# Zero matmuls left out beside the FFN and the prep stage, two loads moved in SyncE's order, a new table of steps

## The chip, the cores and the metric

The kernel runs on one NeuronCore of a Trainium2 chip. The metric is the device time of one execution in microseconds (us); lower is better. All arithmetic is float32 except where bf16 is named.

## The reference, cut to what matters

The model is one hybrid block over `x` of shape (8, 512, 256), that is 8 batch items of 512 positions:

```
x = x + attn(layernorm(x))                      # 16 heads, rotary, causal
x = x + ffn(layernorm(x))                       # FP4-quantised inputs and weights, F = 704
h = layernorm(x)
x = x + (h + mamba(layernorm(h)*gamma + beta))  # two directions, 512 channels, 16 states
x = x + ffn(layernorm(x))                       # the same weights again

# mamba, for each direction:
xc = silu(conv4(xs));  dt = softplus(...)
state = exp(dt*A)*state + dt*B*xc;  y = sum_n state_n*C_n + xc*D     # a scan over 512 positions
y = concat(y_fwd, y_back) @ merge_w * silu(z) @ out_w
```

The scan is the largest single part: 2 directions x 4 tiles of 128 channels x 16 states of a 512-long recurrence for each of 8 batch items.

## The kernel before

**Two streams.** The main stream is the scan. It is cut into units: a unit `K` is two states of one 128-channel tile, so 64 units a block (a block is one batch item) and 512 in all. Per unit ScalarE makes two tiles of factors (L1312), GpSimd the products `dBu` (L1027), VectorE two scans (L891) and two products with C (L898), and TensorE sums the states in a PSUM bank with an identity matmul (`state_sum`, L1614; a float32 matmul is recorded as two instructions). In some units GpSimd adds the two states first (L1038). SyncE spreads the rows of B and C over the 128 partitions for every unit (L544, L556, two transfers of 512 KB).

The side stream is all the rest, for the blocks next door: in the time of block `b` run, in this order, `merge` (end of mamba of block b-1, and the first statistics of item b+1), `ffn` of b-1 (the second FFN, "ffn2"), `latents`, `attention` and `ffn` of item b+1 ("ffn1"), and `prep` of item b+1 (the projection, convolution and inputs of its scan). Each engine has a generator for this side stream; a step of it is a *visit*, the same number on every engine. `VISITS` says how many visits are done at each half unit; `pace(b)` joins the lists of the stages, and each engine's main loop calls `advance(side, visits[2k])` and `advance(side, visits[2k+1])` in unit `k`. Every engine runs its instructions in program order, so this table is the order of the work. The lists give `merge` 5 units, `ffn2` 6, `lat` 8, `att` 22, `ffn1` 5.5, `early` 6.5 (the first 20 visits of prep), and `late` the last 7 visits of prep. After them the block's remaining units run with nothing beside them.

**Zero matmuls.** On TensorE `keep_busy()` (L1359) issues one bf16 matmul of a zero weight tile (`zerob`) with 512 columns, accumulated into the bank of the state sum, so that it adds nothing. It is called once a visit of `ffn` (53 visits) and of `prep` (27 visits), while a state sum is open (`summing[0]`).

**Loads.** SyncE issues all transfers in one queue and waits in order. At visit 0 of `merge` it waits for the stores of the last prep, then loads the input of the next item into `xin` (L471), the gate `yg` (L473) and the residual `x` (L474). VectorE needs `xin` at visit 1 of merge (`tile_stats`, L628), `yg` at visit 3 (L667) and `x` at visit 13 (L674). In `prep` SyncE stores the residual at visit 6 (L497, after GpSimd made it), `xc` of the two directions at 16 and 20 (L504), the gate at 20 (L500), and the dt inputs at 23 and 26 (L510). VectorE's work in an FFN tile runs from the product of gate and up (L705), which waits for TensorE's up matmul, through the quantisation (L595 to L625), to the addition of the result (L726), which waits for the down matmul.

Of the kernel before, what the change touches and what calls it, by code (L numbers as in the profile page):

```python
# [18 lines left out]
BF16 = mybir.dt.bfloat16  # L19
I32 = mybir.dt.int32  # L20

P = 128
B, T, C = 8, 512, 256
TT = T // P
# [16 lines left out]
NP, NQ = 2 * DT, DS // 2  # L41
# [6 lines left out]
YB = 2  # L48
# [94 lines left out]
def mixed_with(i):  # L143
# [6 lines left out]
PREP_EARLY = 20  # L150
EARLY_MERGE = (26, 34, 42, 50, 58)
VISITS = {
    "merge": (1, 1, 1, 1, 0, 5, 0, 2, 2, 5),
    "ffn2": (1, 1, 9, 1, 10, 8, 3, 5, 3, 4, 4, 4),
    "lat": (4, 0, 1, 1, 0, 3, 1, 1, 0, 2, 0, 3, 2, 2, 0, 6),
    "att": (0, 4, 1, 0, 2, 0, 3, 0, 5, 1, 1, 0, 2, 2, 0, 0, 2, 3, 1, 1, 1, 1,
            3, 4, 2, 1, 1, 0, 2, 0, 1, 1, 1, 0, 3, 1, 3, 5, 0, 4, 0, 0, 0, 3),
    "ffn1": (2, 5, 6, 8, 9, 8, 0, 7, 4, 1, 3),
    "early": (4, 1, 2, 1, 2, 0, 5, 1, 1, 0, 3, 0, 0),
    "late": (2, 0, 2, 0, 0, 0, 0, 1, 0, 0, 2, 0, 0, 0, 0),  # L160
}


# [25 lines left out]
def hybrid_block(nc, known, d, out):  # L189

    with ExitStack() as ctx:
        def sb(name, shape, dt=F32):
            return ctx.enter_context(nc.sbuf_tensor("sb_" + name, shape, dt))
# [9 lines left out]
        identb = sb("identb", [P, P], BF16)  # L203
        maskb = sb("maskb", [P, P], BF16)
        cos, sin = sb("cos", [P, T]), sb("sin", [P, T])
        ones = sb("ones", [L + 1, P])
        zerob = sb("zerob", [P, P], BF16)
        e16 = sb("e16", [1, 17])
        w_lat = [[sb(f"w_lat{w}{r}", [P, CK, HL]) for r in range(2)] for w in range(2)]
        b_lat = sb("b_lat", [P, 2 * 2 * MT])  # L210
# [65 lines left out]
        lat = [area(MT, T, start=W), area(MT, T)]  # L276
# [170 lines left out]
        def _(sp):  # L447
# [9 lines left out]
            def merge(c, n):  # L457
                latest = min((c + 2 if n is None else n) - 1, B - 1)
                for v in range(MERGE_N):
                    if v == 0 and c != B - 1:  # L460
                        if latest >= 0:
                            done = 16 * (latest + 1)
                            sp.wait_ge(s_kept_x, done)
                            sp.wait_ge(s_kept_zs, done)
                            for s in range(2):
                                sp.wait_ge(s_kept_xc[s], done)
                                sp.wait_ge(s_kept_z[s], done)
                                sp.wait_ge(s_rows[s], done)
                        if n is not None and n >= 1:
                            sp.wait_ge(V.sem, V.at("attended", n - 1, TT - 1))  # L470
                            sp.dma_start(xin[:, :, :], x_dram[n]).then_inc(s_xin, 16)  # L471
                        if c is not None:
                            sp.dma_start(yg, kept_zs[c]).then_inc(s_yg, 16)  # L473
                            sp.dma_start(x[:, :, :], kept_x[c]).then_inc(s_x, 16)  # L474
                    yield

            def last_loads():
                store_out(B - 2)
# [13 lines left out]

            def prep(n):
                for v in range(PREP_N):
                    if v == 6:
                        sp.wait_ge(G.sem, G.at("residual", n))
                        sp.dma_start(kept_x[n], x[:, :, :]).then_inc(s_kept_x, 16)  # L497
                    if v == 20:
                        sp.wait_ge(A.sem, A.at("z", n, DT - 1))
                        sp.dma_start(kept_zs[n], zs).then_inc(s_kept_zs, 16)  # L500
                    for s, at_xc, at_rows, at_z in ((0, 16, 18, 23), (1, 20, 23, 26)):
                        if v == at_xc:
                            sp.wait_ge(A.sem, A.at("xc", n, s, DT - 1))
                            sp.dma_start(kept_xc[n, s], xc[s]).then_inc(s_kept_xc[s], 16)  # L504
                        if v == at_rows:
                            sp.wait_ge(A.sem, A.at("xds", n, s))
                            sp.dma_start(rows_bc[n, s], xds[s][DR:XD]).then_inc(s_rows[s], 16)
                        if v == at_z:
                            sp.wait_ge(A.sem, A.at("zraw", n, s, DT - 1))
                            sp.dma_start(kept_z[n, s], zraw[s]).then_inc(s_kept_z[s], 16)  # L510
                    yield
# [78 lines left out]
        def _(v):  # L590
# [239 lines left out]
            after(V.n)  # L830
            for r in range(4):
                v.memset(own_rows[L * r:L * r + L, r:r + 1], 1.0).then_inc(V.sem, V.mark())
            v.memset(zerob[:, :], 0.0).then_inc(V.sem, V.mark())
            v.memset(minus_one[:, :], -1.0).then_inc(V.sem, V.mark())
            v.memset(minus_half[:, :], -0.5).then_inc(V.sem, V.mark("cleared"))
            v.wait_ge(s_fold, FOLD)
# [504 lines left out]
        def _(pe):  # L1341
# [9 lines left out]
                if name:  # L1351
                    mm.then_inc(E.sem, E.mark(*name))

            summing = [False]

            def keep_busy():

                if summing[0]:
                    pe.matmul(psum[:, YB], zerob[:, :], identb[:, :].unsqueeze(1).to_broadcast([P, T // P, P]),  # L1359
                              start=False, stop=False)  # L1360

            def merge_tiles(c, first, end):
                for k in range(first, end):
                    pe.wait_ge(V.sem, V.at("ycat", c * NP + k))
# [31 lines left out]

            def ffn(b, f):
                for i in range(FFN_N):
                    keep_busy()
                    for w, first in ((0, 7), (1, 12)):  # L1400
                        if i == first:
                            pe.wait_ge(G.sem, G.at("xq", b, f, w))
# [150 lines left out]

            def prep(n):
                for i in range(PREP_N):
                    keep_busy()
                    if i in (5, 6):
                        k = i - 5
                        pe.wait_ge(A.sem, A.at("normed3", n, TT - 1))
# [42 lines left out]
            def state_sum(K):  # L1602
# [11 lines left out]
                    mm = pe.matmul(psum[:, YB], ident[:, :], dBu[K % SLOTS][:, e],  # L1614
                                   start=(q == 0 and e == 0), stop=(q == NQ - 1 and e == last))
                mm.then_inc(E.sem, E.mark("summed", K))
                summing[0] = q < NQ - 1


            pe.wait_ge(s_fold, FOLD)  # L1620
# [115 lines left out]
```

## Time and profile before

| | |
|---|---|
| median of 3 runs | 3912.75 us (3910.37 to 3913.55) |
| profiled execution, its own time | 3910.42 us |
| its span | 3908.6 us |
| TensorE busy | 3340.3 us (85%), of it the zero matmuls 266.7 us in 842 instructions |
| VectorE busy | 2988.5 us (76%) |
| GpSimd busy | 2136.8 us (55%) |
| ScalarE busy | 1992.6 us (51%) |
| mean granted TensorE clock | 0.945 |

The profiled execution lies 2.3 us below the median, and 1.8 us of it lie outside the span. Matmuls are pipelined, and their busy time contains latency: the distance from start to start is what one of them takes from TensorE. The first scan unit starts at 311.7 us; blocks 1 to 6 start at 717.6, 1179.7, 1642.3, 2104.6, 2571.9 and 3036.9 us, block 7 at 3500.8 us, and its last unit at 3821.2 us. "The granted clock" is a share of the full 2.4 GHz; its two levels are 1 and 0.5.

### The profile page before, as it was taken

The page shows a single profiled execution, that of the slowest core. Times are in us where ns is not written, and L with a number is a line of the kernel's source. Part 1 is how long each engine was busy: PE and PEld are TensorE (multiplying, and loading weights), DVE is VectorE, ACT ScalarE, POOL GpSimd, SP SyncE. Part 2 cuts the span into 40 slices and gives each one's busy share as a digit, 9 for nine tenths or more (in the row PEclk, how much of TensorE's full clock was granted, in tenths as well). Part 3 has the DMA queues.
Part 4 walks back from the last instruction along what each step waited for, and adds up shares of the span by engine and source line. Part 5 has one row for each costly group of instructions (what it writes and reads, how often), then busy time and mean ns, then how long its engine had stood idle before and what let it go on. Part 6 is the DMA issues. An engine that isn't in the chain of part 4 may idle for free.

```text
span 3908.6 us, 40355 instructions
## 1 busy us (share of the span) xinstructions
PE 3340.3 (85%) x12858; PEld 1747.6 (45%) x12858; DVE 2988.5 (76%) x4258; ACT 1992.6 (51%) x3811; POOL 2136.8 (55%) x1333
## 2 busy tenths in 40 slices
PE   7877988899888988889888998889988898889676
PEld 4543543355434554355443454435543455435223
DVE  5346788786887778877887878878688777887885
ACT  2544656346553565545654466534655356553442
POOL 2016566556654665546745466555665466553881
PEclk9988999899999999999999999999999999999888
DMA  3006446644464543734537344464446445373880
GB/s 91 1 28 230 150 136 235 223 146 148 143 239 165 164 162 139 281 112 165 184 116 278 129 148 165 175 224 146 148 142 238 166 159 162 131 283 114 280 273 29
DMA packets 203667, 649.30 MB, mean 166 GB/s; under 512 B 34237, under 2 KB 45504, under 8 KB 197312
## 3 DMA queue, kind: packets, MB, share of 16 engines
q1 hardware_dynamic: 203456, 646.72, 48.8%
q8 instruction: 103, 1.69, 0.2%
q14 instruction: 108, 0.88, 0.1%
HBM read 595.26 MB, written 51.38 MB: 165 GB/s over the span
## 4 chain that ended last, share of the span: by engine, by line
PE 34%; issue 21%; POOL 20%; DVE 16%; ACT 5%; DMA 3%; SPq 1%; POOLq 0%; DVEq 0%; ACTq 0%
PE banks L1345 15%; POOL sb_arena L1027 9%; PE banks L1614 7%; DVE banks L891 5%; PE banks L1385 4%; POOL sb_arena L1038 3%; PE banks L1350 3%; PE banks L1537 3%; DVE sb_arena L898 2%; DVE sb_arena L802 2%; POOL sb_arena L962 2%; ACT banks L1312 2%; POOL sb_arena L939 1%; PE banks L1513 1%; DMA sb_xin<-in_x 1%
## 5 line engine op out<-in xcount | busy, mean ns | idle before, releaser
L1027 POOL TENSOR_TENSOR sb_arena<-sb_arena 128x1024 f32<-128x1024 f32 x512 | 1205.6, 2356 | 364.3 <-DMA sb_arena<-rows_bc 200.3
L891 DVE TENSOR_TENSOR_SCAN banks<-banks,sb_arena 128x512 f32<-128x512 f32 x999 | 1170.0, 1215 | 155.6 <-ACT banks L1312 108.8
L1312 ACT ACTIVATE banks<-sb_arena,sb_neg_a 128x512 f32<-128x512 f32 x1024 | 665.4, 682 | 1014.3 <-DVE sb_arena L898 1003.4
L1614 PE MATMUL banks<-sb_arena,sb_ident 128*128 128x512 f32 x1740 | 915.4, 646 | 277.3 <-DVE sb_arena L898 162.3
L898 DVE TENSOR_TENSOR sb_arena<-banks,sb_arena 128x512 f32<-128x512 f32 x999 | 635.6, 676 | 2.8 <-DMA sb_arena<-rows_bc 2.8
L1614 PEld LDWEIGHTS banks<-sb_arena,sb_ident 128*128 128x128 f32 x1740 | 324.2, 201 | 700.3 <-DVE sb_arena L898 276.9
L1081 ACT ACTIVATE sb_arena<-banks 128x512 f32<-128x512 f32 (+2 forms) x720 | 360.9, 515 | 535.2 <-PE banks L1350 380.8
L1350 PE MATMUL banks<-sb_ident,sb_arena 128*128 128x128 f32 (+1 forms) x2082 | 343.2, 287 | 194.3 <-POOL sb_arena L932 74.0
L756 DVE TENSOR_REDUCE sb_nmax<-banks 128x1 f32<-128x512 f32 (+3 forms) x352 | 223.7, 636 | 270.3 <-PE banks L1540 269.5
L1350 PEld LDWEIGHTS banks<-sb_ident,sb_arena 128*128 128x128 f32 (+1 forms) x2082 | 241.0, 144 | 407.1 <-ACT sb_arena L1081 158.0
L1537 PE MATMUL banks<-sb_arena 128*128 128x384 f32 (+3 forms) x1024 | 353.2, 455 | 1.9 <-POOL sb_arena L949 1.9
L1345 PE MATMUL banks<-sb_w_gu,sb_arena 128*128 128x352 f32 x1024 | 352.8, 493 | 1.5 <-ACT sb_arena L1081 1.5
L939 POOL TENSOR_TENSOR sb_arena<-sb_arena,sb_q_s 128x704 f32<-128x704 f32 x64 | 88.8, 1387 | 477.9 <-DVE sb_arena L625 477.9
L1038 POOL TENSOR_TENSOR sb_arena<-sb_arena 128x512 f32<-128x512 f32 x154 | 195.3, 1268 | 229.6 <-DVE sb_arena L898 227.7
L1157 ACT ACTIVATE sb_arena<-banks,sb_nmax 128x512 f32<-128x512 f32 (+3 forms) x512 | 264.6, 527 | 20.2 <-DVE sb_nmax L756 19.9
L1359 PE MATMUL banks<-sb_identb,sb_zerob 128*128 128x512 bf16 x842 | 266.7, 405 | 0.0
L1345 PEld LDWEIGHTS banks<-sb_w_gu,sb_arena 128*128 128x128 f32 x1024 | 204.6, 204 | 128.3 <-issue 28.6
L1345 PE MATMUL banks<-sb_arena,sb_w_lat 128*128 128x512 f32 x512 | 235.6, 602 | 8.5 <-DVE sb_arena L743 7.8
L1345 PE MATMUL banks<-sb_w_down,sb_arena 128*128 128x256 f32 (+1 forms) x768 | 201.5, 405 | 12.3 <-ACT sb_arena L1081 7.8
L1385 PE MATMUL banks<-sb_arena,sb_w_merge 128*128 128x512 f32 x448 | 196.8, 592 | 0.0
L1513 PE MATMUL banks<-sb_arena 128*32 128x128 f32 x2560 | 183.2, 277 | 6.5 <-ACT sb_arena L1081 6.3
L962 POOL TENSOR_TENSOR sb_arena<-sb_arena,sb_own_rows 128x1024 f32<-128x1024 f32 x64 | 121.3, 1895 | 122.2 <-PE banks L1540 117.7
(130 smaller groups left out, 4102.5 us busy)
## 6 DMA issues: line engine op xcount, KB each, us to landing
sb_arena<-rows_bc SPq DMA_DIRECT2D x1024, 512.0 KB, 4.5
kept_xc<-sb_arena SPq DMA_DIRECT2D x16, 1024.0 KB, 7.6
kept_z<-sb_arena SPq DMA_DIRECT2D x16, 1024.0 KB, 7.5
sb_arena<-kept_xc SPq DMA_DIRECT2D x64, 256.0 KB, 5.1
sb_arena<-kept_z SPq DMA_DIRECT2D x63, 256.0 KB, 5.0
kept_zs<-sb_arena SPq DMA_DIRECT2D x8, 1024.0 KB, 8.6
sb_arena<-kept_zs SPq DMA_DIRECT2D x8, 1024.0 KB, 9.4
sb_xin<-in_x SPq DMA_DIRECT2D x8, 512.0 KB, 7.3
```

Source lines behind the costliest of these rows:

```text
L891: v.tensor_tensor_scan(products if e == 1 and shared(K) else factors, factors, products, 0.0, ALU.mult, ALU.add).then_inc(V.sem, V.mark("s ...
L898: v.tensor_tensor(dBu[K % SLOTS][:, e], psum[:, e], rows_c[K % CS][:, e], ALU.mult).then_inc(V.sem, V.mark("hc", K, e))
L1027: nc.gpsimd.tensor_tensor(dBu[K % SLOTS], u[:, p % 2].unsqueeze(1).to_broadcast([P, 2, T]), rows_b[K % BS], ALU.mult).then_inc(G.sem, G.ma ...
L1038: nc.gpsimd.tensor_tensor(dBu[K % SLOTS][:, 0], dBu[K % SLOTS][:, 0], dBu[K % SLOTS][:, 1], ALU.add).then_inc(G.sem, G.mark("pair", K))
L1081: nc.scalar.activation(dst, src, ACT.Copy).then_inc(A.sem, A.mark(*name))
L1312: nc.scalar.activation(psum[:, e], dt[:, (K // NQ) % 2], ACT.Exp, scale=neg_a[:, s, m, 2 * q + e:2 * q + e + 1]).then_inc(A.sem, A.mark("d ...
L1345: mm = pe.matmul(dst, lhs, rhs, start=(i == 0), stop=(i == len(pairs) - 1))
L1350: mm = pe.transpose(dst, src, ident[0:src.shape[0], 0:src.shape[0]])
L1359: pe.matmul(psum[:, YB], zerob[:, :], identb[:, :].unsqueeze(1).to_broadcast([P, T // P, P]), start=False, stop=False)
L1385: mm = pe.matmul(psum[:, SB[j]], w_merge[:, k, j * P:j * P + P], ycat[:, k], start=(k == 0), stop=(k == 2 * DT - 1))
L1537: pe.matmul(psum[:, bank, e * kl:e * kl + kl], qz[:, m, r], lat[1][:, m, 0:kl], start=(e == 0), stop=False)
L1614: mm = pe.matmul(psum[:, YB], ident[:, :], dBu[K % SLOTS][:, e], start=(q == 0 and e == 0), stop=(q == NQ - 1 and e == last))
```

## The change

The zero matmuls go (TensorE, and the memset of `zerob` on VectorE). The load of `xin` for item n+1 goes from visit 0 of `merge` to visit 0 of `prep(n)`, for the items 2 to 7 (item 1 is still loaded in merge). The load of the residual goes from visit 0 of `merge` to visit 14 of `prep(n)` one block earlier, behind a wait for the store of the newer residual from the same tile. The lists of `VISITS` are other; each stage has as many visits and takes as many half units as before, except that `late` spreads its 7 visits over 8 half units and not 15.

```
 VISITS = {
-    "merge": (1, 1, 1, 1, 0, 5, 0, 2, 2, 5),
-    "ffn2": (1, 1, 9, 1, 10, 8, 3, 5, 3, 4, 4, 4),
-    "lat": (4, 0, 1, 1, 0, 3, 1, 1, 0, 2, 0, 3, 2, 2, 0, 6),
-    "att": (0, 4, 1, 0, 2, 0, 3, 0, 5, 1, 1, 0, 2, 2, 0, 0, 2, 3, 1, 1, 1, 1,
-            3, 4, 2, 1, 1, 0, 2, 0, 1, 1, 1, 0, 3, 1, 3, 5, 0, 4, 0, 0, 0, 3),
-    "ffn1": (2, 5, 6, 8, 9, 8, 0, 7, 4, 1, 3),
-    "early": (4, 1, 2, 1, 2, 0, 5, 1, 1, 0, 3, 0, 0),
-    "late": (2, 0, 2, 0, 0, 0, 0, 1, 0, 0, 2, 0, 0, 0, 0),
+    "merge": (1, 1, 0, 3, 4, 1, 1, 0, 1, 6),
+    "ffn2": (1, 1, 7, 3, 9, 9, 4, 3, 8, 0, 4, 4),
+    "lat": (4, 0, 2, 2, 0, 3, 0, 3, 2, 0, 1, 1, 1, 4, 1, 2),
+    "att": (0, 3, 2, 0, 2, 0, 3, 0, 5, 1, 1, 0, 2, 1, 1, 0, 2, 3, 1, 1, 1, 1,
+            3, 4, 2, 1, 1, 1, 1, 0, 1, 1, 1, 1, 2, 1, 3, 5, 0, 2, 2, 0, 0, 3),
+    "ffn1": (2, 7, 3, 9, 9, 8, 0, 7, 6, 0, 2),
+    "early": (4, 1, 3, 0, 2, 0, 7, 0, 0, 0, 3, 0, 0),
+    "late": (2, 0, 2, 1, 0, 1, 0, 1),
 }
...
-        zerob = sb("zerob", [P, P], BF16)
...
-                        if n is not None and n >= 1:
-                            sp.wait_ge(V.sem, V.at("attended", n - 1, TT - 1))
-                            sp.dma_start(xin[:, :, :], x_dram[n]).then_inc(s_xin, 16)
+                        if n == 1:
+                            load_x(n)
                         if c is not None:
                             sp.dma_start(yg, kept_zs[c]).then_inc(s_yg, 16)
-                            sp.dma_start(x[:, :, :], kept_x[c]).then_inc(s_x, 16)
+            def load_x(n):
+                sp.wait_ge(V.sem, V.at("attended", n - 1, TT - 1))
+                sp.dma_start(xin[:, :, :], x_dram[n]).then_inc(s_xin, 16)
...
             def prep(n):
                 for v in range(PREP_N):
+                    if v == 0 and 1 <= n < B - 1:
+                        load_x(n + 1)
+                    if v == 14 and n >= 1:
+                        sp.wait_ge(s_kept_x, 16 * (n + 1))
+                        sp.dma_start(x[:, :, :], kept_x[n - 1]).then_inc(s_x, 16)
                     if v == 6:
                         sp.wait_ge(G.sem, G.at("residual", n))
                         sp.dma_start(kept_x[n], x[:, :, :]).then_inc(s_kept_x, 16)
...
-            def keep_busy():
-                if summing[0]:
-                    pe.matmul(psum[:, YB], zerob[:, :], identb[:, :].unsqueeze(1).to_broadcast([P, T // P, P]),
-                              start=False, stop=False)
...
             def ffn(b, f):
                 for i in range(FFN_N):
-                    keep_busy()
...
             def prep(n):
                 for i in range(PREP_N):
-                    keep_busy()
```

## Rows read from the trace of the kernel before

**Rows 1.** Windows, one line a block: busy us and count of each engine, clock, DMA.

```profile
717.60:1179.70 462.10, 410.91 (x1602) 216.03 (x1602) 370.26 (x528) 247.04 (x472) 263.95 (x165) 0.96 0.50 173
2104.60:2571.90 467.30, 412.76 (x1602) 216.38 (x1602) 370.24 (x528) 246.89 (x473) 265.52 (x165) 0.96 0.51 171
```

**Rows 2.** Windows of block 3: merge, ffn2, lat, att, ffn1, early, late, last units.

```profile
core 0: us, PE busy (x) PEld busy (x) DVE busy (x) ACT busy (x) POOL busy (x), PEclk, DMA share, GB/s
1642.30:1680.00 37.70, 36.14 (x84) 15.89 (x85) 22.73 (x37) 10.26 (x16) 18.66 (x11) 1.00 0.70 252
...
1752.00:1799.00 47.00, 47.00 (x122) 22.12 (x123) 37.84 (x48) 19.94 (x34) 33.10 (x21) 1.00 0.63 212
...
2013.00:2063.00 50.00, 41.56 (x104) 17.47 (x105) 42.13 (x63) 35.06 (x55) 25.64 (x16) 0.93 0.60 198
...
2084.00:2104.60 20.60, 10.40 (x24) 3.40 (x21) 19.43 (x24) 9.29 (x15) 16.77 (x10) 1.00 0.92 321
```

**Rows 3.** Windows of the merge stages of blocks 1 to 6, and their sum.

```profile
717.60:753.60 36.00, 36.00 (x84) 15.94 (x85) 22.74 (x37) 10.22 (x16) 17.29 (x11) 1.00 0.70 254
...
2104.60:2145.40 40.80, 37.75 (x84) 16.59 (x85) 22.87 (x37) 10.29 (x16) 18.95 (x11) 0.96 0.68 239
...
sum 227.10, PE 218.63 PEld 96.32 DVE 136.80 ACT 61.73 POOL 111.80; mean PE 36.44 PEld 16.05 DVE 22.80 ACT 10.29 POOL 18.63
```

**Rows 4.** Timeline of VectorE, TensorE and SyncE at the start of block 3.

```profile
1645.49 0.38 SPq L471 DMA_DIRECT2D sb_xin<-in_x  x1
...
1653.50 0.75 DVE L628 BATCH_NORM_STATS2 sb_stats<-sb_xin 128x6 f32<-128x256 f32 x2 [6.27 <-DMA sb_xin<-in_x]
...
1650.91 5.31 PE L1385 MATMUL banks<-sb_arena,sb_w_merge 128*128 128x512 f32 x12
1657.78 1.98 PE L1614 MATMUL banks<-sb_arena,sb_ident 128*128 128x512 f32 x4 [1.56 <-DVE sb_arena L898]
```

**Rows 5.** The instructions on the tile `xin`: what they waited for.

```profile
  DMA sb_xin<-in_x: 42.5, 8
```

**Rows 6.** Windows of ffn2 (first three) and of ffn1 in four blocks.

```profile
1216.60:1288.00 71.40, 61.51 (x231) 36.82 (x229) 59.97 (x96) 30.76 (x47) 24.03 (x16) 0.98 0.27 89
1680.00:1751.80 71.80, 61.91 (x231) 37.05 (x229) 60.00 (x96) 30.76 (x47) 24.04 (x16) 0.95 0.26 88
...
2609.70:2682.60 72.90, 64.70 (x231) 37.86 (x230) 60.04 (x97) 30.78 (x47) 24.03 (x16) 0.93 0.26 87
...
1946.20:2012.10 65.90, 58.74 (x206) 32.67 (x206) 56.66 (x91) 31.82 (x48) 30.41 (x23) 0.87 0.30 98
2412.70:2479.20 66.50, 57.45 (x206) 32.43 (x206) 56.72 (x91) 31.82 (x48) 30.47 (x23) 0.92 0.29 96
```

**Rows 7.** Windows of the zero matmuls alone, in ffn2, ffn1 and early.

```profile
1680.00:1751.80 71.80, 12.42 (x42) 4.14 (x42) 0.95 0.26 88
...
1946.20:2012.10 65.90, 16.80 (x50) 5.34 (x50) 0.87 0.30 98
...
2012.10:2062.30 50.20, 6.57 (x21) 2.10 (x21) 0.93 0.60 199
```

**Rows 8.** Timeline of TensorE in FFN stretches.

```profile
1961.35 4.13 PE L1345 MATMUL banks<-sb_w_gu,sb_arena 128*128 128x352 f32 x8
1965.31 0.59 PE L1359 MATMUL banks<-sb_identb,sb_zerob 128*128 128x512 bf16 x2
1965.74 2.53 PE L1345 MATMUL banks<-sb_w_gu,sb_arena 128*128 128x352 f32 x8
1968.11 0.38 PE L1359 MATMUL banks<-sb_identb,sb_zerob 128*128 128x512 bf16 x1
...
1486.51 3.19 PE L1359 MATMUL banks<-sb_identb,sb_zerob 128*128 128x512 bf16 x7
```

**Rows 9.** Groups of VectorE in block 3: busy, mean ns, idle before them.

```profile
L756 DVE TENSOR_REDUCE sb_nmax<-banks 128x1 f32<-128x384 f32 (+3 forms) x44 | 27.9, 634 | 30.6 <-PE banks L1540 30.4
...
L705 DVE TENSOR_TENSOR sb_arena<-sb_arena,banks 128x704 f32<-128x704 f32 x8 | 7.1, 885 | 8.3 <-PE banks L1345 8.3
...
L726 DVE TENSOR_TENSOR sb_x<-sb_x,banks 128x256 f32<-128x256 f32 x8 | 3.3, 418 | 4.9 <-PE banks L1345 4.8
```

**Rows 10.** Timeline of SyncE's queue in prep, block 3.

```profile
2023.53 0.32 SPq L497 DMA_DIRECT2D kept_x<-sb_x  x1
...
2048.34 0.32 SPq L556 DMA_DIRECT2D sb_arena<-rows_bc  x1
2048.71 1.26 SPq L504 DMA_DIRECT2D kept_xc<-sb_arena  x1
```

**Rows 11.** Transfers of the page and of the DMA view: KB each, us to landing.

```profile
kept_x<-sb_x SPq DMA_DIRECT2D x8, 512.0 KB, 4.5
```

More of the change, by code:

```diff
@@ L832, in _ @@
                 v.memset(own_rows[L * r:L * r + L, r:r + 1], 1.0).then_inc(V.sem, V.mark())
-            v.memset(zerob[:, :], 0.0).then_inc(V.sem, V.mark())
             v.memset(minus_one[:, :], -1.0).then_inc(V.sem, V.mark())
@@ L1352, in turn @@
                     mm.then_inc(E.sem, E.mark(*name))
-            summing = [False]
-            def keep_busy():
-                if summing[0]:
-                    pe.matmul(psum[:, YB], zerob[:, :], identb[:, :].unsqueeze(1).to_broadcast([P, T // P, P]),
-                              start=False, stop=False)
             def merge_tiles(c, first, end):
@@ L1616, in state_sum @@
                 mm.then_inc(E.sem, E.mark("summed", K))
-                summing[0] = q < NQ - 1
             pe.wait_ge(s_fold, FOLD)
```

## The prediction, as recorded before the change ran

> **What bounds the kernel now.** I read the windows by block first. Six middle blocks take 462 to 467 us each and hold the same work to within 2 us of VectorE time [rows 1]; so what is won or lost in a block counts about six or seven times. The windows by stage come next, because no engine bounds the whole [rows 2]. In merge TensorE is busy 36.1 of 37.7 us and VectorE only 22.7. In lat TensorE is busy all of 47.0 us. In the last units, with no side work, VectorE is busy 19.4 of 20.6 us and TensorE half. In the two FFN stretches both are near full: TensorE 58.7 and VectorE 56.7 of 65.9 us in ffn1, 61.9 and 60.0 of 71.8 in ffn2 [rows 6]. But TensorE's number there contains the zero matmuls, 16.8 and 12.4 us [rows 7]. Without them it is 41.9 of 65.9 and 49.5 of 71.8 us: there VectorE is the engine to beat, and TensorE matters only where VectorE stands waiting for it. That is read from the groups of VectorE: in a block it waits 8.3 us for up matmuls (L705) and 4.9 us for down matmuls (L726) [rows 9].
>
> **The change part by part.**
>
> *The zero matmuls.* In a run two of them take 0.59 us and one 0.38 us [rows 8], so one more costs 0.21 us of TensorE. In blocks 1 to 6 the two FFN stretches hold 92 of them a block (42 and 50) and early 21 [rows 7]. All of it together is 842 x 0.21 = 177 us, which would be the gain if TensorE set the pace everywhere; the rows above say it doesn't. What lies on the path is what stands, without a pause of TensorE, before a matmul for which VectorE waits. The pattern of a tile shows it: eight gate matmuls from 1961.35, two zeros from 1965.31 to 1965.74, eight up matmuls to 1968.27, and VectorE's L705 follows at once [rows 8]. So 0.43 us of such a wait is zeros. The down matmuls come after two rounds of transposes and copies, in whose pauses the zeros run at no cost. A block has 8 tiles; eight instructions of L705 wait 8.3 us in all [rows 9], and in the timeline all but about one of them do so: 7 x 0.43 = 3.0 us a block, and seven blocks have about this much FFN beside a scan: 21 us. The bounds: 0, if VectorE then waits for something else that is as late; and all of L705's and L726's waits, 13.2 x 7 = 92 us. I take 21, since the pattern is seen, with the zeros of early at 0: there VectorE is busy 42.1 of 50.0 us, TensorE 41.6 [rows 2], and the 21 zeros (4.5 us) mostly lie in TensorE's waits for the convolution. Bounded above by those 4.5 x 7 = 31 us.
>
> *The load of xin.* In block 3 SyncE issues it at 1645.49 and VectorE stands 6.27 us until 1653.50 [rows 4]. In the trace all such waits are 42.5 us in 8 times [rows 5], of which two (item 0 and item 1) stay. But merge is TensorE's stage: while VectorE stands, TensorE works on merge matmuls until 1656.22, and its own wait for VectorE's product is 1.56 us [rows 4]. The six merge stages say the same: the shortest is 36.0 us with TensorE busy all the time, the longest 40.8, and together they take 227.1 us, 11.1 more than six times the shortest [rows 3]. So the gain is 11 us, not the 36 or so of VectorE's waiting; 11 and 36 are the bounds, with 0 as the lower one should the transfer be late at its new place. It isn't: at visit 0 of prep SyncE's wait is for the last addition of attention, a whole FFN earlier, and 17.5 units lie between it and the next merge: early, late and the last units, over 90 us (2012.1 to 2104.6), against 8.0 us from issue to use before [rows 4].
>
> *The load of the residual.* It was in time before, at visit 13 of merge, so by itself it is worth nothing; that merge starts with 1 MB less in flight only helps `yg`. Its new place has a wait, and behind it in SyncE's queue stand the spreads of B and C for the next units, then GpSimd's products, then VectorE. The wait is for the store issued at visit 6, at 2023.53 [rows 10], which lands some 4.5 us later [rows 11]; visit 14 comes two units later. Long done: 0. The two transfers go into a stretch whose DMA share is 0.60 against merge's 0.70 [rows 2]. If they delayed the spreads by their own 8 us, a lead of three units or more (over 20 us here) would cover it. The new list for early puts visits 10 to 16 in one half unit, so SyncE waits for `xc` (L504, at 2048.71 before) ahead of the spreads of one more unit; it already stood until 2048.34 for a spread buffer [rows 10]. I take 0 and keep 1 us a block, 7 us, for it.
>
> *The clock.* This is what speaks against the change. A low clock costs: ffn2 takes 71.4 us at a mean of 0.98, 71.8 at 0.95 and 72.9 at 0.93; ffn1 takes 65.9 us at 0.87 and 66.5 at 0.92, so there it costs nothing visible [rows 6]. The slope in ffn2 is 1.5 us for 0.05. Fewer matmuls mean more idle time for TensorE, and in places nothing but zeros keeps it at work: seven in a row from 1486.51 [rows 8]. On the other side, in the last units of block 3 TensorE is busy half the time and the granted clock is 1.00 [rows 2], while the FFN stretches keep 64% and 69% without zeros. So I expect more falls, not a low stage: the mean in FFN stretches down by 0.03 to 0.04, which by ffn2's slope is 1.0 us each, 14 of them: 14 us lost. Bounds: 0 (ffn1's rows), and the slope applied to a fall of 0.12, 50 us.
> The Trainium skill (TensorE: Matmul & The Clock Gate, "HAM oscillation — how this bites in real kernels") speaks against the change: pauses of TensorE put it back to half clock, so that each burst starts cold. The trace agrees that falls happen beside FFN, but the stage means of 0.87 to 0.98 were had with the fillers in place. By the rule taken strictly, every FFN tile would begin cold; that is the third rival below.
>
> *The table.* Its stages keep their lengths, so the stage bounds stay; only the order inside moves, and `late` ends 1.5 units sooner, where VectorE is the bound and nothing waits. No row gives its price. The largest wait that such an order can touch is VectorE's for attention scores, 30.6 us a block [rows 9]. I take 1 us a block in favour, 7 us, because merge's new list brings TensorE's matmuls forward into the time in which VectorE no longer stands; the bounds are 15 us either way.
>
> The sum against the profiled execution: 3910.4 - 21 - 11 + 14 - 7 = 3885.4; the median of the runs shown is 2.3 us above it, so 3887.7. I forecast 3888 us, 0.6% less.
>
> **The rivals.**
> 1. *VectorE's waits in the FFN go nearly whole.* TensorE then runs ahead in the FFN, and the down matmuls are early too. For it speaks that TensorE has a third of the stretch free; against it, that down matmuls follow copies of ScalarE. Two thirds of the 92 us, 61 instead of 21, and the clock at 14: 3848. Chance 0.15.
> 2. *Nothing comes through.* The zeros ran only in pauses, and the merge stage keeps its length because TensorE was its bound (36.0 us at best). Then 3912.7 - 11 + 14 = 3916, and 3905 at least where the clock costs little and the table pays. Chance 0.17.
> 3. *The clock falls for much of the FFN* (slower). Place: both FFN stretches of every block, where TensorE waits for the quantised tile. It decides from a fall of the mean by 0.09: then 14 x 2.8 us eat the 39 us of all gains. At a fall of 0.12, 3.6 us each: 3912.7 - 39 + 50 = 3924. For it speak the seven zeros in a row, and the skill's rule; against it the half-busy last units at full clock. Chance 0.14.
> My forecast has 0.5; 0.04 is left for a late spread behind the new wait of visit 14, up to +15 us.
>
> **How the numbers follow.** The forecast's own range is 3868 to 3904. A measurement of this kernel tells 0.2%, 8 us, from no change: faster is below 3905, slower above 3920.5. Faster: 0.5 + 0.15 and 0.02 of rival 2, 0.67. Within: most of rival 2 and a part of the others, 0.18. Slower: 0.15. To leave out two in ten the range takes in half of rival 1 and half of rivals 2 and 3: 3848 to 3917.
>
> **What would show it.** Merge stages all near 36 us, without VectorE's wait for xin. FFN stretches 1 to 2 us shorter, L705's wait in a block down from 8.3 to about 5 us. Their granted clock 0.03 to 0.04 lower; at 0.80 rival 3 holds. Lat unchanged at 47 us. Wrong I would be by the table above all, since it has no price, and by the clock where slow matmuls fall on waits of VectorE.

## The result, and the profile after

The changed kernel takes 3952.35 us (median of 5 runs, 3948.61 to 3956.88) against 3912.75 us before (3910.37 to 3915.54 in its 5 runs beside it). The ratio is 1.0099, with a 95% interval of 1.0088 to 1.0111: 1.0% slower, where 3888 us and 0.6% less was forecast. The profiled execution has a span of 3946.8 us and a mean granted clock of 0.922; before it was 3908.6 us and 0.945.

First the windows by block, as in [rows 1] (columns: window and length, then busy us and count on TensorE, its weight loads, VectorE, ScalarE, GpSimd, then granted clock, DMA share, GB/s).

```profile
720.30:1186.80 466.50, 388.28 (x1480) 206.78 (x1480) 372.37 (x528) 247.06 (x472) 264.95 (x165) 0.94 0.50 171
...
1657.90:2129.60 471.70, 393.54 (x1481) 209.82 (x1481) 372.34 (x528) 247.24 (x473) 265.64 (x166) 0.92 0.50 170
```

TensorE has lost its ballast (388 to 394 us a block for 406 to 413), VectorE's work is 2 us more (372.4 for 370.2 in block 1), and yet a block takes 1.5 to 9.4 us more; the two shown, blocks 1 and 3, take 4.4 and 9.4. The six middle blocks sum to 2814.3 us (720.3 to 3534.6) for 2783.2 before (717.6 to 3500.8), so 31 of the 38 us of span lie there. The windows of block 3 by stage show where: merge, ffn2, lat, att, ffn1, early, late, last units.

```profile
1657.90:1693.90 36.00, 36.00 (x84) 16.05 (x85) 23.04 (x37) 10.34 (x17) 18.92 (x12) 1.00 0.62 232
1693.90:1767.80 73.90, 57.62 (x189) 35.09 (x187) 59.89 (x96) 30.77 (x47) 26.80 (x18) 0.88 0.28 98
1767.80:1823.50 55.70, 55.62 (x134) 26.64 (x135) 39.77 (x50) 19.94 (x35) 35.32 (x24) 0.91 0.50 164
1823.50:1966.20 142.70, 126.67 (x773) 75.96 (x771) 109.30 (x149) 97.42 (x241) 101.17 (x63) 0.99 0.51 167
1966.20:2033.00 66.80, 46.04 (x156) 27.70 (x156) 58.44 (x91) 31.60 (x48) 30.50 (x23) 0.87 0.30 97
2033.00:2083.90 50.90, 38.07 (x85) 16.81 (x85) 42.88 (x64) 34.45 (x54) 24.46 (x15) 0.87 0.65 207
2083.90:2105.30 21.40, 19.52 (x43) 7.12 (x41) 18.26 (x21) 12.57 (x22) 9.91 (x6) 1.00 0.96 350
2105.30:2129.60 24.30, 14.00 (x21) 4.45 (x21) 20.76 (x24) 10.16 (x17) 18.56 (x11) 0.79 0.87 289
```

And lat and the last units of block 3 in the kernel before:

```profile
1751.80:1798.30 46.50, 46.41 (x121) 21.79 (x121) 37.14 (x47) 19.46 (x33) 33.24 (x22) 1.00 0.63 213
...
2082.10:2104.60 22.50, 12.30 (x27) 4.21 (x27) 21.10 (x25) 11.16 (x18) 18.18 (x11) 1.00 0.93 315
```

Merge is at 36.0 us with TensorE busy throughout, as the shortest was in [rows 3]; the wait for the input is gone. Everything else but att is longer. ffn2 takes 73.9 us at a clock of 0.88 where block 3 had 71.8 at 0.95 [rows 6]. Lat takes 55.7 for 46.5 us (47.0 in the slightly wider window of [rows 2]), att 142.7 for 147.9; how these two belong together is shown below. The last units, with hardly any side work, take 24.3 us at a clock of 0.79 for 22.5 at 1.00. The groups of VectorE in this block, beside [rows 9]:

```profile
L711 DVE TENSOR_TENSOR sb_arena<-sb_arena,banks 128x704 f32<-128x704 f32 x8 | 7.1, 882 | 5.7 <-PE banks L1350 4.7 <-ACT sb_arena L1108 1.0
...
L732 DVE TENSOR_TENSOR sb_x<-sb_x,banks 128x256 f32<-128x256 f32 x8 | 3.4, 420 | 11.5 <-PE banks L1350 11.3
```

The wait for up matmuls (now L711) fell from 8.3 to 5.7 us, where about 5 was forecast. The wait for down matmuls (now L732) rose from 4.9 to 11.5 us, and it takes back more than was won. Block 3 is one of the worst; over the six middle blocks the first wait went from 54.2 to 39.4 us and the second from 29.6 to 57.6. Not all of this is the zeros' doing: the experiments below share it out between them and the table. The timeline of TensorE and VectorE at one such wait in ffn2 shows why, with the windows of the three microseconds before the down matmuls and of the four that they begin in:

```profile
1733.18 4.66 PE L1350 MATMUL banks<-sb_w_down,sb_arena 128*128 128x256 f32 x12 [0.52 <-ACT sb_arena L1086]
...
1737.87 0.42 DVE L732 TENSOR_TENSOR sb_x<-sb_x,banks 128x256 f32<-128x256 f32 x1 [1.88 <-PE banks L1350]
...
1730.00:1733.00 3.00, 1.10 (x6) 0.59 (x6) 2.83 (x5) 2.20 (x5) 0.82 (x1) 1.00 0.45 150
1733.00:1737.00 4.00, 3.82 (x10) 2.97 (x10) 2.86 (x5) 1.41 (x2) 0.00 (x0) 0.57 0.06 23
```

Ahead of the twelve down matmuls TensorE had waited 1.06, 0.69 and 0.52 us, with two zero matmuls before in each such place and nothing now. They run mostly at the lower of the two levels (1.2 GHz; mean 0.57) and take 4.66 us, and VectorE stands 1.88 us for them. In the kernel before, the same place of the first ffn2 tile of block 3 looks like this:

```profile
1719.41 0.44 PE L1350 MATMUL banks<-sb_ident,sb_arena 128*128 128x128 f32 x2 [0.26 <-ACT sb_arena L1081]
1719.68 0.59 PE L1359 MATMUL banks<-sb_identb,sb_zerob 128*128 128x512 bf16 x2
1720.37 3.05 PE L1345 MATMUL banks<-sb_w_down,sb_arena 128*128 128x256 f32 x12
```

The trace has 48 such groups of twelve down matmul instructions in the six middle blocks, and each takes 3.05 us. In the changed kernel 34 of the 48 do, and 14 take 4.5 to 5.8 us.

### The profile page after: what moved, and what is told of

It reads as the page before. It is cut to its first block, busy times and chain, and to the rows that moved or that the text cites. A ratio compares the mean times of both kernels' runs of the same rounds, so it can differ in the third digit from the quotient of the medians.

```text
span 3946.8 us, 38670 instructions
## 1 busy us (share of the span) xinstructions
PE 3195.7 (81%) x12016; PEld 1694.1 (43%) x12016; DVE 3003.5 (76%) x4257; ACT 1993.5 (51%) x3811; POOL 2136.2 (54%) x1333
## 4 chain that ended last, share of the span: by engine, by line
PE 42%; POOL 20%; issue 16%; DVE 14%; ACT 5%; DMA 2%; SPq 1%; POOLq 0%; DVEq 0%; ACTq 0%
PE banks L1350 19%; POOL sb_arena L1032 10%; PE banks L1609 8%; PE banks L1382 5%; PE banks L1355 3%; DVE banks L896 3%; PE banks L1533 3%; POOL sb_arena L1043 3%; DVE sb_arena L808 2%; DVE sb_arena L903 2%; DMA sb_arena<-rows_bc 2%; PE banks L1509 2%; ACT sb_arena L1086 1%; POOL sb_arena L967 1%; ACT banks L1317 1%
## 5 line engine op out<-in xcount | busy, mean ns | idle before, releaser
L1609 PE MATMUL banks<-sb_arena,sb_ident 128*128 128x512 f32 x1740 | 931.7, 657 | 299.8 <-DVE sb_arena L903 185.5
L1355 PE MATMUL banks<-sb_ident,sb_arena 128*128 128x128 f32 (+1 forms) x2082 | 352.1, 293 | 311.1 <-POOL sb_arena L937 129.3
L1350 PE MATMUL banks<-sb_w_gu,sb_arena 128*128 128x352 f32 x1024 | 342.5, 490 | 8.6 <-ACT sb_arena L1086 6.2
L1350 PE MATMUL banks<-sb_w_down,sb_arena 128*128 128x256 f32 (+1 forms) x768 | 229.5, 448 | 33.4 <-ACT sb_arena L1086 33.4
L1350 PEld LDWEIGHTS banks<-sb_w_down,sb_arena 128*128 128x128 f32 (+1 forms) x768 | 157.9, 219 | 96.6 <-ACT sb_arena L1086 51.6
L1350 PE MATMUL banks<-sb_arena,sb_w_in 128*128 128x512 f32 x256 | 135.9, 679 | 63.7 <-DVE sb_arena L808 62.6
```

The costliest lines, as they stand in the source:

```text
L1350: mm = pe.matmul(dst, lhs, rhs, start=(i == 0), stop=(i == len(pairs) - 1))
L1355: mm = pe.transpose(dst, src, ident[0:src.shape[0], 0:src.shape[0]])
```

## The experiments

Medians beside runs of the kernel before on the same chip, whose own medians were 3912.6 to 3915.7 us. In this table "clock" is the mean of the profiled execution.

| run | what differs from the kernel before | median us | ratio, 95% interval | clock |
|---|---|---|---|---|
| e1_no_zeros | zeros out | 3930.89 | 1.0038 (1.0019 to 1.0056) | 0.928 |
| e2_loads | loads moved | 3900.47 | 0.9966 (0.9954 to 0.9978) | 0.945 |
| e3_table | new table | 3938.36 | 1.0064 (1.0049 to 1.0078) | 0.945 |
| e4_new_zeros | loads and table | 3938.59 | 1.0066 (1.0052 to 1.0079) | 0.947 |
| e5_lat_att | new lists lat, att | 3911.30 | 0.9994 (0.9985 to 1.0003) | 0.947 |
| e6_ffn_lists | new lists ffn2, ffn1 | 3936.49 | 1.0053 (1.0041 to 1.0066) | 0.945 |
| e7_prep_lists | new lists early, late | 3936.05 | 1.0050 (1.0037 to 1.0064) | 0.944 |
| e8_merge_list | new list merge | 3898.21 | 0.9962 (0.9950 to 0.9975) | 0.949 |
| e9_ffn2_tail | 4 entries of ffn2 | 3921.92 | 1.0023 (1.0013 to 1.0033) | 0.947 |
| e10_early_bunch | 3 entries of early | 3934.73 | 1.0053 (1.0040 to 1.0066) | 0.946 |
| e11_double_zeros | two zeros a visit | 3980.55 | 1.0174 (1.0161 to 1.0188) | 0.957 |
| e12_loads_merge | loads moved, new list merge | 3900.46 | 0.9965 (0.9953 to 0.9976) | 0.952 |
| e13_zeros_ffn_only | zeros out beside prep | 3914.46 | 1.0005 (0.9995 to 1.0014) | 0.942 |
| e14_zeros_prep_only | zeros out beside the FFN | 3931.59 | 1.0048 (1.0029 to 1.0067) | 0.931 |
| e15_zeros_head | FFN zeros at visits 0 to 11 only | 3945.15 | 1.0078 (1.0062 to 1.0093) | 0.932 |
| e16_after_old_lists | changed kernel, old FFN and prep lists | 3923.12 | 1.0029 (1.0018 to 1.0040) | 0.918 |
| e17_zeros_128 | zeros of 128 columns | 3927.57 | 1.0026 (1.0016 to 1.0036) | 0.929 |
| e18_zeros_256 | zeros of 256 columns | 3917.55 | 1.0007 (0.9997 to 1.0017) | 0.932 |

### The three parts, one at a time

```
e1:  in ffn and in prep
-                    keep_busy()
e2:  the hunks of the diff in SyncE's merge and prep, nothing else
e3:  VISITS of the changed kernel in the kernel before
e4:  e2 and e3 together (the changed kernel with its zeros put back)
```

> The kernel before with the zero matmuls left out and nothing else changed (table and loads as before). Theory clock (TensorE, emptied beside FFN and prep, falls to half clock more often, and the slow down matmuls hold VectorE): about 40 us slower than before, 3950 us, mean granted clock 0.92, VectorE's wait for down matmuls up from 4.9 to about 11 us a block. Theory table (the new table is the loss, the zeros were ballast): 3890 us, 20 us faster than before.

> The kernel before with only the two loads moved into prep. Both theories: the merge stages of blocks 1 to 6 all at 36 us, 11 us faster than before, 3902 us. If the loads at their new place delay the spreads of B and C: same as before or slower, with early and late longer.

> The kernel before with only the new table of steps (zeros and loads as before). Theory clock: within 10 us of before, 3905 to 3920 us, since the zeros still hold the clock. Theory table: 30 us or more slower, with lat longer than 46.5 us.

> The changed kernel with the zero matmuls put back, so new table and moved loads together. Theory clock: 3895 to 3905 us, faster than before, the clock back at 0.945. Theory table: 3940 us or more, the zeros changing nothing.

Neither theory held alone. The zeros cost 17 us when left out, under half of the loss; the table costs 25 us with the zeros in place and the clock unchanged at 0.945; the loads bring 13 us. The three do not add to the 39.6 us that the change cost (17 - 13 + 25 = 29). The odd one is the loads: with the old table they bring 13 us, with the new one nothing (3938.59 against 3938.36). From e4 to the changed kernel, which differ in the zeros alone, it is 13.8 us. So the change, taken in this order, is 25 for the table, 0 for the loads on top of it, 14 for the zeros. In another order the loads would have their 13 and the table more.

### The table, list by list

```
e5:  lat and att of the new table     e6:  ffn2 and ffn1     e7:  early and late
e8:
-    "merge": (1, 1, 1, 1, 0, 5, 0, 2, 2, 5),
+    "merge": (1, 1, 0, 3, 4, 1, 1, 0, 1, 6),
```

> The kernel before with only the lists lat and att of the new table. In the kernel with the whole new table lat is 5.4 us longer and att 5.0 us shorter in each middle block. Theory boundary (the two only trade work over their border): within 5 us of before. Theory lat list is the loss: 15 to 25 us slower.

> The kernel before with only the lists ffn2 and ffn1 of the new table. Both stages are 1.1 and 0.7 us longer with the whole new table. Theory lists (bunched visits are the loss, stage by stage): about 12 us slower. Theory whole-table (only the lists together lose): no difference.

> The kernel before with only the lists early and late of the new table. Theory lists: early 1.2 us, late 1.4 us and the last units 0.3 us longer in each of seven blocks, 15 to 20 us slower. Theory boundary: no difference.

> The kernel before with only the list merge of the new table, the loads in merge as before. With the whole new table the merge stage is 1.5 us shorter than before without any load moved. Theory: the new list alone already hides the wait for the input, about 8 us faster than before. Rival: the shorter merge stage there is bought by a longer ffn2, no difference.

e5 is within 0.1% of before: the 5 us that lat gains in every block att gives back, so that part of the stage table above is a border moved. It is 5.4 us in lat (51.9 for 46.5, in e5 as in four blocks of the changed kernel). Block 3 has 9.2, and block 2 too: there the last down matmuls of ffn2 run into lat at the low clock, which e5 doesn't have.

```profile
1767.88 5.78 PE L1350 MATMUL banks<-sb_w_down,sb_arena 128*128 128x256 f32 x12 [0.52 <-ACT sb_arena L1086]
```

The FFN lists cost 22 us (expected 12), the prep lists 22 (expected 15 to 20), and the merge list brings 16 (expected 8). The sum, +22 +22 -16 and 0 or -3 for e5, is the 25 us of the table.

e8 says why the loads bring nothing on top. Its timeline at the start of block 3, beside [rows 4]:

```profile
1653.93 0.75 DVE L628 BATCH_NORM_STATS2 sb_stats<-sb_xin 128x6 f32<-128x256 f32 x2 [6.77 <-DMA sb_xin<-in_x]
...
1650.83 7.89 PE L1385 MATMUL banks<-sb_arena,sb_w_merge 128*128 128x512 f32 x18
1658.56 1.88 PE L1614 MATMUL banks<-sb_arena,sb_ident 128*128 128x512 f32 x4
```

VectorE still stands 6.77 us for the input. But TensorE has 18 merge instructions before its next state sum, where it had 12, and waits for nothing. Merge takes 35.9 us, TensorE's own time. Hiding a wait of the engine that isn't the bound was worth as much as removing it.

### Single bunches of visits

```
e9:
-    "ffn2": (1, 1, 9, 1, 10, 8, 3, 5, 3, 4, 4, 4),
+    "ffn2": (1, 1, 9, 1, 10, 8, 4, 3, 8, 0, 4, 4),
e10:
-    "early": (4, 1, 2, 1, 2, 0, 5, 1, 1, 0, 3, 0, 0),
+    "early": (4, 1, 2, 1, 2, 0, 7, 0, 0, 0, 3, 0, 0),
e12:  e2 with the new list merge
```

> The kernel before with one change in the table: entries 7 to 10 of ffn2 are 4, 3, 8, 0 and not 3, 5, 3, 4. With both new FFN lists, units 8 to 10 of a block take 36.1 us and before 34.6. Theory bunch (eight FFN visits in one half unit and none in the next leave the scan waiting): 1.4 us a block, about 10 us slower than before. Theory head (the loss comes from the first half of the lists): no difference.

> The kernel before with one change in the table: early has 7, 0, 0 where it had 5, 1, 1; late as before. Theory bunch: unit 50 grows by 2 us and unit 51 gives back 1.9, the stage 1 us longer, 7 to 12 us slower than before. Theory late (the loss of the prep lists comes from late's visits being a unit earlier, which brings the 1 MB store of the dt inputs nearer the load of the input): no difference here.

> The kernel before with the moved loads and the new list merge, zeros and all other lists as before. Each alone takes 13 to 16 us off. Theory same wait (both remove TensorE's stand behind VectorE's wait for the input, and merge is at its floor of 36 us in both): together 3898 us, no better than one. Theory additive: 3885 us.

The swap in early costs 19 us (expected 7 to 12), nearly all of the 22 us of both prep lists. The timeline of e10 around unit 50 of block 3, with the same place of the kernel before under it:

```profile
2041.77 13.44 DVE L802 SCALAR_TENSOR_TENSOR sb_arena<-banks,sb_w_conv,sb_arena 128x509 f32<-128x509 f32 x18 [1.10 <-ACT sb_arena L1176]
2050.81 3.61 PE L1345 MATMUL banks<-sb_arena,sb_w_in 128*128 128x512 f32 x4 [6.71 <-DVE sb_arena L802]
...
2058.07 1.30 ACT L1312 ACTIVATE banks<-sb_arena,sb_neg_a 128x512 f32<-128x512 f32 x2 [7.58 <-DVE sb_arena L898]
2058.86 2.34 DVE L891 TENSOR_TENSOR_SCAN banks<-banks,sb_arena 128x512 f32<-128x512 f32 x2 [0.23 <-ACT banks L1312]
```

```profile
2033.68 8.99 DVE L802 SCALAR_TENSOR_TENSOR sb_arena<-banks,sb_w_conv,sb_arena 128x509 f32<-128x509 f32 x12 [1.10 <-ACT sb_arena L1176]
...
2042.73 3.65 PE L1345 MATMUL banks<-sb_arena,sb_w_in 128*128 128x512 f32 x4 [4.99 <-DVE sb_arena L802]
...
2047.75 1.30 ACT L1312 ACTIVATE banks<-sb_arena,sb_neg_a 128x512 f32<-128x512 f32 x2 [5.34 <-DVE sb_arena L898]
```

Seven visits in one half unit put 18 convolution steps on VectorE in a row where there were 12, 13.44 us for 8.99. No product with C comes between, so ScalarE, which needs it for the next factors, waits 7.58 us for 5.34, and TensorE waits 6.71 for 4.99. In the middle blocks early is 1.0 us longer, late 1.6, and merge 0.7. How the last two follow from the first was not tested. The changed kernel has the same run in block 3:

```profile
2054.93 13.44 DVE L808 SCALAR_TENSOR_TENSOR sb_arena<-banks,sb_w_conv,sb_arena 128x509 f32<-128x509 f32 x18 [1.10 <-ACT sb_arena L1181]
```

e9 costs 7 us (expected 10). Units 8 to 10 of the profiled block, first of e9, then of the kernel before:

```profile
1719.90:1756.10 36.20, 33.45 (x130) 19.31 (x128) 30.45 (x43) 17.03 (x30) 12.12 (x7) 1.00 0.24 80
```

```profile
1717.20:1751.80 34.60, 32.90 (x129) 19.17 (x127) 30.43 (x43) 16.98 (x29) 10.99 (x6) 1.00 0.25 84
```

The same work of VectorE takes 1.6 us longer at the same full clock; this part of the loss isn't the clock. VectorE's wait for down matmuls goes from 29.6 to 36.4 us in the six middle blocks, and it is 36.4 in e3, e4 and e6 too. The other 15 us of the FFN lists were not traced to an entry. e12 confirms the shared wait: both cures together are no better than either, 3900 us.

### The zeros, by place and by size

```
e11:
                 if summing[0]:
+                    for _ in range(2):
-                    pe.matmul(psum[:, YB], zerob[:, :], ...)
+                        pe.matmul(psum[:, YB], zerob[:, :], ...)
e13:  prep without keep_busy()      e14:  ffn without keep_busy()
e15:  in ffn
-                    keep_busy()
+                    if i < 12:
+                        keep_busy()
e16:  the changed kernel with ffn2, ffn1, early and late of the old table
e17:  pe.matmul(psum[:, YB, 0:P], zerob, identb)            # 128 columns
e18:  pe.matmul(psum[:, YB, 0:2 * P], zerob, identb twice)  # 256 columns
```

> The kernel before with two zero matmuls a visit where it had one, nothing else. Theory clock: the granted clock goes up from 0.945 to about 0.955, but TensorE has another 0.2 us a visit to carry: 3900 to 3920 us. Theory ballast (zeros cost what they occupy, and the clock doesn't matter): as far above before as leaving them out would be below, so 3930 us or more with the kernel without zeros at 3890; that kernel has been seen at 3931, so then both directions lose and one zero a visit is near the best.

> The kernel before without the zero matmuls beside prep, those beside the FFN kept. Theory clock in prep (the loss of about 17 us without any zeros lies in early and in what follows it): 8 to 12 us slower. Theory FFN: no difference, within 4 us.

> The kernel before without the zero matmuls beside the FFN, those beside prep kept. Theory clock in prep: 5 to 10 us slower at most. Theory FFN: 15 us slower, as without any zeros, with the clock of the FFN stages down.

> The kernel before with the zero matmuls of an FFN only at its first 12 visits (before and between the two groups of input transposes, where TensorE waits for the quantised input), none beside the four tiles; prep as before. Theory fill (zeros in TensorE's waits hold the clock, zeros between gate and up are ballast on the path): 10 to 20 us faster than before. Theory dose (each zero helps the clock about as much as it costs): within 8 us of before.

> The changed kernel (no zeros, loads moved) with the lists ffn2, ffn1, early and late of before; its own merge, lat and att lists stay. If the parts add up: 3914 + 17 for the zeros - 15 for loads and merge list together, 3916 us, about 36 us faster than the changed kernel. If the bunched lists only cost where zeros are there: 3940 us or more.

> The kernel before with zero matmuls of 128 columns and not 512, same count and places. Theory clock (what counts is how long the zeros keep TensorE at work): near the kernel without zeros, 3925 to 3932 us, granted clock 0.930 to 0.935. Theory order (their mere presence between other matmuls matters): near before, within 5 us.

> The kernel before with zero matmuls of 256 columns. Theory clock: between, 3915 to 3925 us, granted clock near 0.94. If the on-path time that halves (about 1.5 us a block) outweighs a clock that mostly holds: 3905 us, faster than before.

By place: without zeros beside prep nothing is lost (1.0005), without those beside the FFN it is 19 us, as without any. So my theory of prep was wrong. e15 was the larger miss: I had taken the zeros between gate and up for ballast and expected 10 to 20 us of gain from dropping all but the first twelve visits'; it is 32 us slower, no better than no FFN zeros at all. The zeros beside the tiles are those that pay. Whether the head ones alone do harm isn't settled: the six runs of e15 (3933 to 3951 us) and of e14 (3918 to 3949) overlap.

By size, all at the same places: with 0, 128, 256, 512 and 1024 columns a visit the medians are 3930.9, 3927.6, 3917.6, about 3914 and 3980.6 us, with clocks of 0.928, 0.929, 0.932, 0.945 and 0.957 (for 256 columns 0.94 was expected). That a matmul stands there does little; how long it runs does. From 512 up the sign turns though the clock goes on rising. The groups of twelve down matmuls follow the same order. Counted in the one profiled execution of each run, in the six middle blocks, all with the old table:

| run | groups of 48 that take over 4 us | this execution, us |
|---|---|---|
| before | 0 | 3910.4 |
| e18, 256 columns | 7 | 3916.8 |
| e17, 128 columns | 12 | 3922.6 |
| e1, none | 13 | 3924.0 |
| e14, none beside the FFN | 14 | 3926.8 |
| e15, head only | 16 | 3933.0 |

No run with zeros of 512 or 1024 columns at every visit of the FFN has a single such group, with the old table or the new one. One of e1's, which takes 3.05 us in the kernel before:

```profile
1991.57 4.74 PE L1345 MATMUL banks<-sb_w_down,sb_arena 128*128 128x256 f32 x12 [0.52 <-ACT sb_arena L1081]
```

The FFN windows of block 3 show both sides, ffn2 then ffn1, first with no zeros (e1), then with two a visit (e11); [rows 6] lies between.

```profile
1693.50:1765.00 71.50, 56.60 (x189) 34.12 (x187) 59.90 (x96) 30.79 (x47) 24.02 (x16) 0.88 0.25 88
1959.30:2025.90 66.60, 49.10 (x153) 29.17 (x154) 57.49 (x91) 31.70 (x48) 31.23 (x23) 0.82 0.29 98
```

```profile
1706.70:1781.10 74.40, 69.09 (x272) 40.88 (x271) 60.05 (x96) 30.75 (x47) 24.47 (x17) 0.98 0.24 85
1975.90:2048.30 72.40, 66.33 (x256) 37.98 (x256) 56.98 (x91) 31.88 (x48) 30.99 (x23) 0.93 0.26 91
```

With two zeros TensorE is busy 66.3 of 72.4 us in ffn1, and the stage grows by 6.5 us: there it has become the bound. With none the clock of ffn1 falls to 0.82 and that of ffn2 to 0.88, TensorE is free for 5 and 10 us more than in [rows 6] (14.9 for 9.9 in ffn2, 17.5 for 7.2 in ffn1), and the stages move by less than 1 us.

And the groups of VectorE in block 3 of e1:

```profile
L705 DVE TENSOR_TENSOR sb_arena<-sb_arena,banks 128x704 f32<-128x704 f32 x8 | 7.1, 882 | 7.7 <-PE banks L1345 7.7
...
L726 DVE TENSOR_TENSOR sb_x<-sb_x,banks 128x256 f32<-128x256 f32 x8 | 3.4, 419 | 6.7 <-PE banks L1345 6.6
```

Against 8.3 and 4.9 in [rows 9]: 0.6 us won on up matmuls, 1.8 lost on down matmuls. The six middle blocks together say it more fairly: 41.6 us for 54.2 on up matmuls and 43.2 for 29.6 on down matmuls, 12.6 won and 13.6 lost. That is an even exchange. It explains why the gain of the forecast didn't come, but not the 17 us. The span of e1's profiled execution is 13.6 us longer: 7.0 in the middle blocks (5.0 of it in their merge stages, 232.1 for 227.1), 4.1 in block 0, and 3.5 before the first unit, with 1 us less at the end. These 3.5 aren't the zeros': the first zero matmul of the kernel before runs at 539.8 us, and the start of the first unit varies from 310.5 to 314.7 us among the other runs. How the rest comes about isn't shown.

With the new table the exchange is not even. From e4 to the changed kernel, where the zeros alone differ, the wait for up matmuls goes from 47.4 to 39.4 us and that for down matmuls from 36.4 to 57.6: 8.0 won, 21.2 lost, a net 13.2 us beside the 13.8 measured (the middle blocks take 9.4 us more).

The kernel without zeros also spreads from 3915.1 to 3944.9 us over its 9 runs, the kernel before beside it from 3906.2 to 3925.0 over 15; its single profile (3924.0) lies 7 us below its median, so pieces this small are not certain.

e16 is the changed kernel without the bunched lists: 3923.1 us, 29 us faster than the changed kernel (36 expected) and 7 us above the sum expected.

## Why the prediction was wrong

**The table** is the step that failed most. I wrote that no row gives its price, took 7 us in its favour with 15 either way, and it costs 25 (e3 against before). A row could have warned: VectorE's convolution run L802 of 8.99 us already stood on the path, with ScalarE and TensorE waiting 5.34 and 4.99 us for its end, and the new list put two more visits into just that half unit. I read that list only for SyncE's queue. That the merge list "brings TensorE's matmuls forward" was right, and it is worth 16 us alone, but only about 2 on top of the loads (e12 beside e2); the FFN and prep lists lose 22 each, and the two swaps tested, e10 and e9, are 26 of these 44. The sign "Lat unchanged at 47 us" failed by the table too, by the border that e5 shows.

**The zero matmuls on the path.** The zeros do stand in L705's wait, but the term was too large. It was to fall by some 3 us a block, to about 5; with the zeros alone out (e1) it fell by 0.6 in block 3 and by 2.1 in the mean. The 14.8 us that it lost over six blocks in the changed kernel are 6.8 for the new lists (54.2 to 47.4 in e4, which has the zeros) and 8.0 for the zeros. And I compared the wait only with itself. What it gave VectorE, the down matmuls took: over the six middle blocks of e1, 13.6 us for 12.6. Of the 11.5 us for 4.9 in block 3 of the changed kernel, 1.2 is the lists' (6.1 in e4) and 5.4 comes with the zeros gone. "In whose pauses the zeros run at no cost" was true, and was also what made them useful.

**The clock** is the term that was mis-sized. I expected the mean of the FFN stretches to fall by 0.03 to 0.04. In e1 it fell from 0.95 to 0.88 in ffn2 and from 0.87 to 0.82 in ffn1 of block 3; in the mean of the six middle blocks from 0.94 to 0.90 and from 0.91 to 0.83. So ffn2 fell as forecast and ffn1 by twice as much. My evidence against more was the last units, half busy at full clock, and I had read them in block 3, the only one where this held: in the other five the clock was 0.85 to 0.93 with the zeros in place, and in the changed kernel it is 0.72 to 0.87, with 144.1 us for 137.3 in the six. The price by the slope of ffn2, 1.5 us for 0.05, was wrong as well: ffn2 of e1 is 71.3 us at 0.90 in the mean for 72.3 at 0.94. The mean clock of a stage doesn't say which matmuls ran slow. Together, zeros and clock were priced at -7 us and measured +17 (e1) and +14 (e4 to the changed kernel).

The rule of the Trainium skill drawn on there (TensorE: Matmul & The Clock Gate, "HAM oscillation — how this bites in real kernels") is that pauses of TensorE bring back the low clock and a burst after them starts cold. The trace agrees in kind: the twelve down matmuls behind three pauses ran at a mean of 0.57 and took 4.66 us for 3.05. It doesn't agree in extent: the page's pauses are waits of 3 to 5 us for a transfer, the longest before this group was 1.06 us, and in the changed kernel 14 of 48 such groups ran slow, not every one.

**The loads** were right: 11 us forecast, 13 measured alone (e2), merge at 36 us in all six blocks, no delay behind the new wait. That the table's merge list cures the same wait I did not see, so the 11 us were counted for the loads and the list's help besides. With the new table in place the loads bring nothing (e3 and e4).

**The rivals.** The third, slower by the clock, had its sign and mechanism; it asked for a fall of 0.09 in all FFN stretches (0.07 and 0.04 were seen in e1) and gave 3924 us for one of 0.12. The 1.0% have it as the smaller part, and the table, which no rival priced, as the larger. Nothing of rival 1 was seen. From the forecast of 3888 us to the 3952 measured it is 64 us: 32 for the table (+25 for -7), 21 for zeros and clock (+14 for -7), 11 for the loads (0 for -11). The range, 3848 to 3917, stopped 35 us short; the table's bound of 15 us, a guess, accounts for 10 of them.

The fastest versions are e8 (one line of the table, 3898.2 us) and, within the spread of each other, e2 and e12 (3900.5): 0.34 to 0.38% below before.

## What to carry to other kernels

Filler work on an engine is judged at two places: at the wait it lengthens and at the work that follows the pauses it filled, and the second can't be read from its own rows. In an order written by hand, look for the longest run of side work between two steps of the main recurrence and for who waits at its end; moving two visits there cost 19 us, while moving work across a stage border cost nothing. Price a cure by the engine that bounds the stage: two cures of one wait bring one gain.

## What the runs showed of the hardware

The granted clock and the time part ways on both sides. Doubling the zeros raised the mean clock from 0.945 to 0.957 and cost 65 us against the kernel before on the same chip (3980.6 for 3915.4), and fillers of 256 columns held the time within 0.2% at a mean of 0.932, not much above the 0.928 of none at all. Of two kernels with a mean of 0.932 in the profiled execution one takes 3917.6 us and the other 3945.2 (e18 and e15; 7 and 16 slow groups of down matmuls), and e16, at 0.918, is faster than e1 at 0.928 (3923.1 and 3930.9, though with another table and other loads). Where the low clock falls counts for more than how much of it there is.

The clock also fell where no pause was long. In the three microseconds before one such fall TensorE was busy 1.10 us and its longest pause was 1.06 us; with two zero matmuls in each of these pauses it didn't fall there.
